# A state-space, routing and delta-rule kernel: start of the Mamba phase reordered, solve and state update of the delta phase split anew

## What is computed

```python
x = x + mamba(layernorm(x))      # 1: selective scan, 512 inner channels, 16 states, window-4 convolution
x = x + experts(layernorm(x))    # 2: 32 experts, each takes its 8 best tokens
x = x + delta_rule(layernorm(x)) # 3: 8 heads of 32, chunks of 32 tokens
x = x + experts(layernorm(x))    # 4: as 2
```

```python
# 1
delta = softplus(dBC[..., :64] @ W_dt.T + b_dt)
h[l]  = exp(delta[l] * A) * h[l-1] + delta[l] * B[l] * xc[l]
y[l]  = sum_n(h[l] * C[l]) + Dp * xc[l];  out = (y * silu(z)) @ W_out.T
# 3, per head and chunk
T = inverse(I + strict_lower(beta * k @ k.T))      # 32x32, by rows
u = T @ (beta * v) - (T @ (beta * k)) @ S
o = q @ S + lower(q @ k.T) @ u;  S = S + k.T @ u
```

## Time and profile before

| | us |
|---|---|
| median of 3 runs (lowest, highest) | 2192.84 (2190.7, 2193.0) |
| the profiled execution: time, span | 2187.78, 2185.9 |
| Mamba phase: start of phase to first scan | 81.7 |
| Mamba phase: first scan to last sums | 975.3 |
| delta phase: first solve to last solve begun | 479.2 |
| delta phase: the rest of it | 80.9 before, 98.2 after |
| busy share of the span: PE, PEld, DVE, ACT, POOL | 56%, 26%, 68%, 40%, 54% |

### The profile page before, as it was taken

One profiled execution on the slowest core, in us unless ns is written; L12 is line 12 of the kernel. 1 busy time (PEld: TensorE's weight loads), 2 busy tenths in 40 slices (PEclk: granted clock), 3 DMA queues, 4 the chain that ended last, 5 costly groups with the idle time before them and its releaser, 6 DMA issues. The chain is left out here.

```text
span 2185.9 us, 33415 instructions
## 1 busy us (share of the span) xinstructions
PE 1224.3 (56%) x13720; PEld 576.7 (26%) x13720; DVE 1489.9 (68%) x1766; ACT 880.6 (40%) x1586; POOL 1181.2 (54%) x547
## 2 busy tenths in 40 slices
PE   4364646645564655543375536565666666456655
PEld 1111212121121312120232213233444344332322
DVE  2598988989888988889651123777878787717112
ACT  4465464645556474644122205434334442012120
POOL 0688879888888979889501001434554356512100
PEclk8575777677686677765598877667777777567988
DMA  2917255282716446280489951011221122119997
GB/s 70 224 34 174 57 135 126 73 188 50 182 30 162 98 102 149 50 199 13 122 348 382 397 197 40 20 41 50 70 59 32 50 60 60 41 49 374 335 383 297
DMA packets 195622, 301.84 MB, mean 138 GB/s; under 512 B 84176, under 2 KB 126672, under 8 KB 179088
## 3 DMA queue, kind: packets, MB, share of 16 engines
q1 hardware_dynamic: 192240, 297.29, 45.9%
q0 software_dynamic: 2304, 2.37, 0.5%
q10 hardware_dynamic: 928, 0.07, 0.0%
HBM read 257.21 MB, written 42.47 MB: 137 GB/s over the span
## 5 line engine op out<-in xcount | busy, mean ns | idle before, releaser
L347 POOL TENSOR_TENSOR state<-dx_rep,b_rep 128x2048 f32<-128x2048 f32 x128 | 577.7, 4523 | 64.8 <-issue 47.5
L562 DVE TENSOR_TENSOR_SCAN psum<-psum,state 128x1024 f32<-128x1024 f32 x160 | 365.9, 2287 | 59.0 <-POOL state L347 37.3
L692 PE MATMUL psum<-state,sel 128*32 128x512 f32 x1024 | 192.5, 840 | 347.1 <-POOL state L354 338.5
L446 ACT ACTIVATE psum<-delta_rep,a_neg 128x511 f32<-128x511 f32 x512 | 331.1, 684 | 67.0 <-DVE state L562 66.8
L354 POOL TENSOR_TENSOR state<-state,c_rep 128x1024 f32<-128x1024 f32 x96 | 225.6, 2350 | 89.7 <-DVE state L562 89.6
L562 DVE TENSOR_TENSOR_SCAN state<-psum,state 128x1024 f32<-128x1024 f32 x96 | 218.7, 2278 | 18.3 <-ACT psum L446 18.3
L628 PE MATMUL psum<-xt,w_in 128*128 128x512 f32 x256 | 171.8, 832 | 58.8 <-DVE x_conv L531 37.0
L569 DVE TENSOR_TENSOR state<-psum,c_rep 128x1024 f32<-128x1024 f32 x160 | 195.8, 1224 | 5.5
L818 POOL DMA_DIRECT2D moe_b<-in_w x64 | 33.0, 522 | 254.0 <-DVE moe_xt L969 253.4
L443 ACT COPY psum<-zeros 128x2 f32<-128x2 f32 x160 | 26.3, 164 | 338.4 <-DVE state L569 338.3
L1529 DVE SCALAR_TENSOR_TENSOR conv_qkv<-xpad_qkv,conv_w_qkv,conv_qkv 128x512 f32<-128x512 f32 x144 | 118.1, 885 | 47.9 <-ACT conv_qkv L1422 47.9
(11 more groups left out here) (208 smaller groups left out, 2518.6 us busy)
## 6 DMA issues: line engine op xcount, KB each, us to landing
moe_w_set<-in_w SPq DMA_DIRECT2D x32, 4096.0 KB, 36.1
delta_rep<-delta_scratch SPq DMA_DIRECT2D x128, 256.0 KB, 4.6
dx_rep<-dx_scratch SPq DMA_DIRECT2D x128, 256.0 KB, 7.4
b_rep<-bc_scratch SPq DMA_DIRECT2D x32, 256.0 KB, 4.8
c_rep<-bc_scratch SPq DMA_DIRECT2D x32, 256.0 KB, 7.6
delta_scratch<-delta SPq DMA_DIRECT2D x32, 256.0 KB, 2.0
dx_scratch<-delta_x SPq DMA_DIRECT2D x32, 256.0 KB, 8.0
moe_x<-x_after SPq DMA_DIRECT2D x16, 512.0 KB, 11.1
```

Source lines behind the costliest of these rows:

```text
L347: nc.gpsimd.tensor_tensor(ring[q % RING][:, :, :], dx_rep[u % CHUNKS][:, :, :], free_bcast(b_rep[q // QPB % 2][:, g, :], 1, CB), ALU.mult) ...
L446: ins = nc.scalar.activation(dec[:, i, 1:], delta_rep[u % CHUNKS][:, c, 1:], ACT.Exp, scale=a_neg[:, dt * CB + c, g:g + 1])
L562: nc.vector.tensor_tensor_scan(bx if by_pool(k) else flat, flat, bx, 0.0, ALU.mult, ALU.add).then_inc(S["scan_done"], 1)
L692: ins = nc.tensor.matmul(bank[32 * c:32 * c + 32, :], sel[:, :], ring[q % RING][:, c, :], start=False, stop=(g == NG4 - 1), skip_group_che ...
```

## The change

**Mamba phase.** The ring is 5 quads, and POOL multiplies by C three quads behind its inputs (before two). The parameters have four semaphores, and each reader waits for its own. In batch 0 the four tiles of the input projection go into four banks, SiLU and softplus go tile by tile, the z projections and the second batch's norm are moved behind the dt projections (the z part on ACT into k = 2 and 4), and SP loads chunk 0 as soon as tile 0 is stored. In later batches SP stores the tiles in pairs and loads chunk 0 between them. All side work of PE stands one quad earlier; `gate_y` stands one half later, `add_output` two halves later (i = 9), one half ahead of the taps of i = 10, whose projection waits for it.

**Delta phase.** `solve_below` is cut by halves so that products with zero blocks are left out: DVE has 2048 products in each part, POOL 1024, after a copy of the second diagonal block in transposed order (`copy_second`, 256 elements), and POOL's part 1 waits for DVE's part 0. -v is put into the bank by PE (`minus_vn`, a product with -I), K S is added to it, ACT copies y, and u is copied with scale -1. The state's four 32x32 diagonal blocks are copied, two by DVE and two by ACT; the zeros around them are set once. The slots are new: projections of a unit in m = 0 to 4 of its front iteration (only the first in m = 15 before), statistics in 7, token tiles in 10 and 11, Gram matrices in 12 and 14, masks in 13 and 14, the tail in 5 to 7, and the solve in 0, 4, 5, 7, 8, 10. Parameters are loaded in parts, some from ACT's queue.

```diff
-    RING = 4
+    RING = 5
...
                 store_bc(0)
-                load_bc(0)
+                sp.wait_ge(S["bc_stored"], 16)
+                load_replicated(0, 0)
                 for t in range(DT):
                     store_delta(0, t)
-                for t in range(DT):
                     store_dx(0, t)
-                load_chunk(0, 0)
-                load_chunk(0, 1)
+                    if t < 2:
+                        load_chunk(0, t)
+                    if t == 0:
+                        load_replicated(0, 1)
                 for b in range(B):
                     load_chunk(b, 2)
...
-                        for t in range(DT):
-                            store_delta(b + 1, t)
-                        for t in range(DT):
-                            store_dx(b + 1, t)
-                            if t < 2:
-                                load_chunk(b + 1, t)
+                        for pair in ((0, 1), (2, 3)):
+                            for t in pair:
+                                store_delta(b + 1, t)
+                            for t in pair:
+                                store_dx(b + 1, t)
+                            if pair[0] == 0:
+                                load_chunk(b + 1, 0)
...
-                    if q >= 2:
-                        for k in (2 * q - 4, 2 * q - 3):
+                    if q >= 3:
+                        for k in (2 * q - 6, 2 * q - 5):
                             if by_pool(k):
                                 times_c(k)
...
+                xt_copies(0)
+                act.wait_ge(S["pads_zero"], 3)
+                act.wait_ge(S["conv_loaded"], 16 * 2)
+                for t in range(DT):
+                    last_tap(0, t)
+                conv_silu(0)
+                nc.scalar.preload_act_table_set("natural_log_exp_and_others")
+                copy_dbc(0)
+                act.wait_ge(S["proj_loaded"], 16 * 3)
+                for t in range(DT):
+                    softplus_parts(0, (t,))
                 act.wait_ge(S["params_loaded"], 16 * N_PARAMS)
                 for j in range(NJ):
                     rows = slice(32 * j, 32 * j + 32)
...
+                    if k == 1:
+                        norm_root(1)
+                    if k in (2, 4):
+                        for t in (0, 1) if k == 2 else (2, 3):
+                            z_silu(0, t)
+                        nc.scalar.preload_act_table_set("natural_log_exp_and_others")
+                    if k == 5:
+                        norm_apply(1)
...
-                    if i % 8 == 3 and k >= 8:
...
+                    if i % 8 == 4 and k >= 8:
...
-                    if i == 7 and n >= 2:
+                    if i == 9 and n >= 2:
...
-                    n, i = q // QPB + 1, q % QPB
+                    n, i = (q + 1) // QPB + 1, (q + 1) % QPB
...
+        def below_times_first(s, top, pr):
+
+
+            t_lane, n_lane = t_lanes[s % 2], n_lanes[s % 2]
+            rows, j0 = (slice(0, QC), 0) if top else (slice(QC, HC), QC)
+            pr = pr[:, :].rearrange("p (k m j) -> p k m j", k=QC, m=HC)
+            return (pr, free_bcast(t_lane[:, rows, j0:HC], 2, HC), free_bcast(n_lane[:, HC:C, j0:HC], 1, QC),
                     x_lane[:, rows, :])
...
+            t_lane = t_lanes[s % 2]
+            c0, m1 = (QC, HC) if right else (0, QC)
+            pr = pr[:, :].rearrange("p (k i m) -> p k i m", k=HC, i=QC)
+            return (pr, free_bcast(x_lane[:, :, 0:m1], 2, QC), free_bcast(t22_lane[:, c0:c0 + QC, 0:m1], 1, HC),
+                    t_lane[:, 0:HC, HC + c0:HC + c0 + QC])
+
+        def state_blocks(g):
+
+            rows = slice(g * DK, (g + 1) * DK)
+            return (banks.whole[rows, 2:2 + NP, 0:KD * DK].rearrange("r p (h e) -> r p h e", e=DK), state[rows, :, :, rows])
 
...
+                    if solve is not None:
+                        solve_below(solve, 0)
+                        solve_below(solve, 1)
...
+                        n, phase = m // 4, m % 4
+                        if chain is not None:
+                            k = CT * c + n
+                            if phase == 0 and k % SPG:
+                                act.wait_ge(S["x_chunk"], with_state(k))
+                                nc.scalar.copy(y[:, :], u_bank[:, 0:D]).then_inc(S["y_ready"], 1)
+                            if phase == 1:
+                                act.wait_ge(S["u_psum"], k + 1)
+                                nc.scalar.activation(u[:, :], u_bank[:, 0:D], ACT.Copy,
+                                                     scale=-1.0 if k % SPG else 1.0).then_inc(S["u_ready"], 1)
+                            if phase == 2 and k % SPG != SPG - 1:
+                                act.wait_ge(S["s_psum"], leaving_state(k))
+                                for g in (2, 3):
+                                    blocks, place = state_blocks(g)
+                                    ins = nc.scalar.copy(place, blocks)
+                                ins.then_inc(S["s_ready_act"], 1)
+                        if front is not None and m < 5:
+                            last_tap(f, m + 1)
...
+                def copy_second(s):
+                    ch = Chain(dve, S["solve"], SOLVE * s + 2 * (HC - 1))
+                    ch.wait()
+                    if s:
+                        dve.wait_ge(S["solve_pool"], SOLVE_POOL * s)
+                    ch.step(nc.vector.tensor_copy(t22_lane[:, :, :], t_lanes[s % 2][:, HC:C, HC:C].rearrange("p m i -> p i m")))
...
-                            if phase == 0 and k % SPG:
-                                dve.wait_ge(S["x_chunk"], with_state(k))
-                                dve.wait_ge(S["vn_ready"], c + 1)
-                                nc.vector.tensor_tensor(y[:, :], vns[c % COPIES][:, n, :], u_bank[:, 0:D],
-                                                        ALU.subtract).then_inc(S["y_ready"], 1)
...
-                                for hh in range(KD):
-                                    blocks = banks.whole[:, 2:2 + NP, hh * DK:(hh + 1) * DK]
-                                    ins = nc.vector.tensor_tensor(
-                                        state[:, :, hh, :].rearrange("r p (g e) -> r p g e", e=DK), free_bcast(blocks, 2, HS),
-                                        free_bcast(head_mask[:, :].rearrange("r (g e) -> r g e", e=DK), 1, NP), ALU.mult)
+                                for g in (0, 1):
+                                    blocks, place = state_blocks(g)
+                                    ins = nc.vector.tensor_copy(place, blocks)
...
+                        if solve is not None and m == 0:
+                            for row in range(1, 6):
+                                solve_row(solve, row)
+                        if front is not None and m == 1:
+                            taps(f, (0, 1))
...
+                        if solve is not None and m in (4, 5):
+                            for row in (range(6, 9) if m == 4 else range(9, 12)):
+                                solve_row(solve, row)
...
+                        if solve is not None and m == 7:
+                            for row in range(12, HC):
+                                solve_row(solve, row)
+                            copy_second(solve)
...
+                        if front is not None and m in (13, 14):
...
+                def minus_vn(k):
+                    pe.wait_ge(S["vn_ready"], k // CT + 1)
+                    pe.wait_ge(S["u_ready"], k)
+                    nc.tensor.matmul(u_bank[:, 0:D], neg_ident[:, :], vns[k // CT % COPIES][:, k % CT, :], start=True, stop=False,
+                                     skip_group_check=True)
...
+                            if m == 0 and k % SPG:
+                                minus_vn(k)
...
+                            if phase == 3 and m != SLOTS - 1:
+                                minus_vn(k + 1)
                         if front is not None:
-                            if m in (0, 1):
-                                project(f, 4 + m)
-                            if m == 3:
-                                statistics(f)
...
-                            if m == 4:
+                            if m < 5:
+                                project(f, m + 1)
+                            if m == 7:
+                                statistics(f, 2 * (tail + 1) if tail is not None else 0)
+                            if m == 8:
                                 statistics_to_tokens(f)
+                        if tail is not None:
                             if m == 5:
-                                gram(f, 0)
-                            if m == 7:
-                                gram(f, 1)
-                            if m == 9:
-                                for n in range(CT):
-                                    to_tokens(f, n)
-                        if tail is not None:
-                            if m == 10:
```

(23 more changed lines are left out.)

502 lines of the change are left out of this document (255 added, 247 removed).

## The result

The changed kernel takes 2079.83 us (median of 4 runs, 2075.59 to 2083.51), the kernel before beside it 2192.92. The ratio is 0.9485 (95% interval 0.9464 to 0.9507): 113 us faster. Forecast were 147, to 2045. A second measurement of the same kernel (`k12_control`), later and on the same chip as two others, gave 2084.79 and 0.9517 (0.9487 to 0.9547), so the gain is 109 to 113. The profiled execution took 2075.59, its span is 2073.9.

The account below looks back on a forecast made before the run. DVE was taken to set Mamba's pace, and the order of instructions the delta phase's, where no engine is full. Mamba -61 and delta -86 from 2187.8 gave 2041, near 2045 as a median; forecast band 2005 to 2088, range 1998 to 2106.

Parts of the forecast that it names:

- Start of Mamba: Start to first scan: from 81.7 to 55.6 us, 26 us earlier, with bounds 22 and 31.
- Batches: Mamba batches: POOL's lateness (26.8 us) and nearly all `add_output` waits (27.8) go, decay waits stay; six batches -32, the last -6.
- Delta, DVE's work: Delta iteration: DVE has 14.1 us less work, from corner -7.0, y -1.5, state -2.1 and taps -3.5.
- my reading of 8.46: Delta corner: the 8.46 us product is slow from reading T strided; copied first, it goes like the other, 2.25 each.
- The 1 us charged for the lock: Delta iteration: DVE and POOL take turns for SBUF in the corner's products, charged at 1 us an iteration.
- Waits: Delta iteration: 13.9 us of old DVE waits replaced by 9 for N's store and read-back plus 9 for other waits.
- The doubled 2.27 and the 4.57: Delta iteration: K' u behind Gram products (2.27) counted twice, K S behind statistics on PE (4.57) stays; 9 us in all.
- Ends: Delta phase's ends: start -6 us (0 to -12), last stretch -19 (-8 to -28).
- A: Delta phase: the new order gains nothing, an iteration stays at 71 us; 2102, 2107 as a median; chance 13%.
- B: Waits hidden better: stalls of 3 instead of 9 us, cheap end of other bounds; 1993, 1998 as a median; 9%.
- C: Delta phase: PE, slow after pauses, becomes the bound at 84.5 us an iteration; 2214, 2219 as a median; chance 5%.
- D: Whole kernel: loads held up by bandwidth in Mamba and no delta-order gain; gains shrink under 4.4 us; chance 2%.

Follow-up runs that it names:

- k1_shift_on_act: Norm shift (-mean*rstd) of Mamba batches 1 to 7 moved from DVE to small ACT instructions, against the changed kernel: 2078.66 us, ratio 0.9469 to the kernel before.

## Why the prediction was right, and where it was short

**The sign and the main mechanisms** were right: both phases gained, the time is in the band of 2005 to 2088 that had 71%, and the likeliest time was 35 too low. Terms of both sums were mis-sized, and one was missing.

**Start of Mamba**: 26 forecast, 21.8 measured, just under the lower bound of 22. The projection came at 13.52 (forecast 13.4), the first softplus at 34.99 (32.0), the chunk load 8.5 later (7.5), the scan 16.4 after that (16.1). The step that failed is the path to the softplus: its end was counted as "table load, SiLU of the last tile and dt projection 3.8", but dBC's eight products stand in it, 6.33 us from 26.77. They took 3.60 before; now PE had paused 3.66 ahead of them, its granted clock over them is 0.57 (1.00 before), and the 2.7 us between are most of the 3.0 lost; at the 3.60 of before the softplus would have come at an estimated 32.3:

```profile
26.77 6.33 PE L689 MATMUL psum<-x_conv,w_x 128*96 128x512 f32 x8 [3.66 <-ACT x_conv L424]
```

```profile
26.77:33.10 6.33, 6.33 (x8) 2.03 (x8) 1.82 (x6) 2.81 (x4) 0.00 (x0) 0.57 0.00 0
```

**Batches**: the 26.8 and 27.8 us went, the decays stayed (37.1), the taps wait 2.8 (I took 3). The failed step is one that the sum did not have: DVE's norm shift now begins beside a POOL instruction. It took 13.9 us in seven instances (about 1 before), and the kernels without it are 8 faster in this phase. From first scan to the experts' load 35 less was forecast, 27 came, and 37 without the shift (`k1_shift_on_act`, 952.8 for 989.6): the rest of this sum was right. Before, POOL waited 89.6 us for DVE's scans and began behind the shift; now it waits 0.6 for them and 93.4 for PE. Which part of the change did that, no run isolates.

**Delta, DVE's work**: taps 12.3 for 15.9, as forecast (-3.5); state -1.4 (-2.1) and y -1.2 (-1.5), since the iteration that was read has three of each and not the four that I counted. The corner is 11.3 (1.8 of it the standing named below), not 9.9: both parts of my reading of 8.46 were off. "Copied first, it should go like the other" held, but not because the stride had cost 3.3 ns an element; it had cost 1.8, and POOL the rest. The 1 us charged for the lock was too little: 1.8 in the corner, 1.6 in a solve row, 2.1 at the gates, 5.5 an iteration. I had put half of one row's excess; in these rows DVE waits for all that is left of POOL's instruction.

**Waits**: 18 forecast, 14.6 measured (7.29, 0.54, 0.51, 6.29). N's 9 was right in size (7.3 to 9.1). Its round trip by the rows, store issued 1623.09 and row at 1631.51, is 8.4. The Trainium skill, page DMA: Bandwidth & Descriptors, section "Anatomy of one DMA", gave an estimate of 6.4; its figures are for DMAs issued from GpSimd, these are issued from SP, and the row decides. It was only half the cause: with the taps in front of N, the wait for the projection costs the same. The doubled 2.27 and the 4.57 did not come at their old places; 6.3 at the second Gram pair, which I did not name, came instead.

So an iteration is 50.2 of work (44 forecast) and 14.6 of waits (18): 64.8 for 62, and 63.4 to 68.8 for the four full ones. That 64.8 is near 62 is partly luck: the work was 6 too low and the waits 3 too high. Ends: the start -12 (-6), the last stretch -15 (-19) and, in the control, -13.

**Rivals.** A (nothing gained in delta) is excluded by 59 to 63 us, though its reason, no single bound to shorten, is what the runs with less work or moved waits show. B needed stalls of 3, and the wait for N alone is 7.3 to 9.1. C did not come as a whole: PE's granted clock rose, 0.79 for 0.72 over the solves, and PE is busy 48.3 of 64.8. But its slow products behind a pause are there, at the start of Mamba and behind the masks. D is excluded.

**Open**: why the delta phase of one code varies from 601 to 613, where the one of before took 666.0 and 665.5. The granted clock over the solves is 0.79 to 0.80 in all of these, so it does not tell them apart. PE's pauses that no event ends come to 13 to 16 us at the Gram products (L1859 of the changed kernel) in two of these executions, but no run isolates them. Nor does a run hold the clock behind the masks and change nothing else, so what the slow projection costs is not shown. No run takes back the edits of the delta phase one by one (state blocks, -v on PE, the slots), nor those of the start: their shares of the gain are read from traces and not tested.

## What to carry to other kernels

When a change moves two engines against each other, look at the first engine's short instructions with all operands in SBUF: what they lose stands in their duration, not in a wait. Where every engine has slack, neither less work nor an earlier piece shortens anything until something useful stands under the wait that closes the loop. Find what is released by the same event as that wait before calling the wait the cost, and read the granted clock of what PE does behind a pause before putting a price on it.

## What the runs showed of the hardware

- Some DVE instructions whose tensors all lie in SBUF last until the running POOL instruction ends: 4.52 us for 0.14 (two inputs), 1.83 for 0.26 (two inputs, 98 elements), 1.74 for 0.18 (one input, 128x64). Reductions (2.286 us in all kernels), the reciprocal (0.55) and scans with an operand in PSUM (2.28) kept their time. POOL also stands for DVE: its first two additions behind the second corner product took 3.98 us together, and 5.45 where DVE's product was 1.5 longer.
- Reading one operand at a stride of 32 floats cost 1.73 to 1.84 ns an element, for 1.11.
- Eight products took 6.69 us behind 1.6 us of a waiting PE, at a granted clock of 0.50 and then 0.60; four of the same kind right behind others took 1.98, at 1.00. The same eight products of 128x512 for dBC took 6.33 us at 0.57 and 3.60 at 1.00.
